# Expert outputs of the last three groups: scattered by token and loaded plainly, in place of gathers and pauses on GpSimd

## The reference, cut to what matters

```python
logits = xf @ gate_w + gate_b
probs = softmax(logits)
top2_vals, top2_idx = top_k(probs, 2)
cw = zeros((N, 8)).at[arange(N)[:, None], top2_idx].add(top2_vals)
for e in range(8):
    h = gelu(xf @ W1[e] + b1[e])
    out += cw[:, e:e+1] * (h @ W2[e] + b2[e])
```

## Time and profile before

| | |
|---|---|
| Median of 3 runs | 3025.66 us (3024.79 to 3034.64) |
| The profiled execution's own time | 3015.32 us |
| Its span, from the first to the last instruction | 3013.5 us |
| TensorE, busy | 2478.9 us, 82% of the span |
| VectorE, busy | 1969.8 us, 65% |
| ScalarE, busy | 1863.8 us, 62% |
| GpSimd, busy | 1698.9 us, 56% |
| Granted TensorE clock, mean | 0.929 of full speed |

### The profile page before, as it was taken

How to read it: one execution, slowest core, us unless ns; L and a number is a source line. 1 busy time by engine, 2 the same in 40 slices (tenths; PEclk the granted TensorE clock), 3 DMA queues, 4 the chain that set the end, 5 groups by cost and what they waited for, 6 DMA issues and landing times.

```text
span 3013.5 us, 75982 instructions
## 1 busy us (share of the span) xinstructions
PE 2478.9 (82%) x27338; PEld 1745.8 (58%) x27338; DVE 1969.8 (65%) x5155; ACT 1863.8 (62%) x3409; POOL 1698.9 (56%) x1758
## 2 busy tenths in 40 slices
PE   6898888988999888888988998888988877675720
PEld 3566556666666666566666666666666665554510
DVE  3688878887666667877777777677777775422222
ACT  3666666667776667677677677767777754432310
POOL 1224455544333334655555565555567778689986
PEclk9999999999999999899999999999999998787965
DMA  5233443336444454334433343333354443456743
GB/s 214 103 116 121 165 166 128 132 125 220 164 163 139 138 184 145 112 106 123 129 111 114 110 151 115 122 112 115 122 155 123 133 135 119 131 177 212 229 129 92
DMA packets 262562, 421.90 MB, mean 140 GB/s; under 512 B 41756, under 2 KB 141224, under 8 KB 261424
## 3 DMA queue, kind: packets, MB, share of 16 engines
q1 hardware_dynamic: 219376, 327.69, 32.0%
q0 software_dynamic: 32768, 67.17, 7.9%
q10 hardware_dynamic: 10048, 22.19, 2.3%
HBM read 198.26 MB, written 231.22 MB: 143 GB/s over the span
## 4 chain that ended last, share of the span: by engine, by line
PE 51%; ACT 18%; POOL 12%; issue 9%; DVE 5%; DMA 3%; SPq 2%; ACTq 1%; POOLq 0%; DVEq 0%
PE bank_m L844 8%; POOL yg L1238 7%; PE bank_to L768 5%; PE bank_m L836 4%; PE bank_s L808 4%; PE bank_s L736 3%; PE bank_s L814 3%; PE bank_s L723 3%; ACT pt_sb_a L1064 3%; PE bank_to L777 3%; ACT v_a L1049 2%; ACT L1194 2%; POOL xin L1248 2%; PE bank_s L746 2%; ACT p_sb_b L1069 2%
## 5 line engine op out<-in xcount | busy, mean ns | idle before, releaser
L1228 POOL DMA_INDIRECT x_sorted<-xn_c,place_i x512 | 534.3, 1044 | 338.5 <-PE bank_s L707 121.1
L1238 POOL DMA_INDIRECT yg<-y_sorted,place_i x512 | 517.0, 1010 | 277.7 <-PE bank_to L790 131.9
L1221 POOL TENSOR_TENSOR s_sb_a<-s_sb_a,mx_a 128x512 f32<-128x512 f32 x256 | 266.9, 1043 | 674.4 <-DVE mx_a L1614 674.0
L1606 DVE TENSOR_TENSOR s_sb_a<-bank_s,bias_a 128x512 f32<-128x512 f32 x256 | 176.5, 689 | 314.9 <-PE bank_s L707 219.8
L836 PE MATMUL bank_m<-xe,wk_e 128*128 128x512 f32 x552 | 276.3, 625 | 38.7 <-ACT hid L1099 29.0
L844 PE MATMUL bank_m<-wk_e,hid 128*128 128x128 f32 x2208 | 281.6, 290 | 0.9 <-ACT hid L1099 0.9
L1221 POOL TENSOR_TENSOR s_sb_b<-s_sb_b,mx_b 128x512 f32<-128x512 f32 x256 | 271.6, 1061 | 11.9 <-DVE mx_b L1614 11.9
L844 PEld LDWEIGHTS bank_m<-wk_e,hid 128*128 128x128 f32 x2208 | 275.8, 207 | 2.0 <-issue 1.9
L768 PE MATMUL bank_to<-k_consts,p_sb_b 128*128 128x128 f32 x1024 | 173.1, 293 | 103.4 <-ACT pt_sb_a L1064 68.9
L1069 ACT ACTIVATE p_sb_a<-s_sb_a 128x512 f32<-128x512 f32 x256 | 160.7, 628 | 128.4 <-POOL s_sb_a L1221 128.1
L1099 ACT ACTIVATE hid<-bank_m,wk_e 128x512 f32<-128x512 f32 x276 | 183.9, 686 | 74.1 <-PE bank_m L836 66.5
(11 more groups left out here) (222 smaller groups left out, 5920.8 us busy)
## 6 DMA issues: line engine op xcount, KB each, us to landing
y_sorted<-t_back SPq DMA_DIRECT2D x192, 512.0 KB
y_sorted<-yo SPq DMA_DIRECT2D x170, 256.0 KB
wk_e<-in_w_experts_dram SPq DMA_DIRECT2D x134, 321.0 KB
xs<-x_sorted SPq DMA_DIRECT2D x134, 256.0 KB
t_kept<-t SPq DMA_DIRECT2D x64, 256.0 KB
t_back<-t_kept SPq DMA_DIRECT2D x32, 512.0 KB
xin<-in_x_dram SPq DMA_DIRECT2D x128, 112.0 KB
x_res<-in_x_dram SPq DMA_DIRECT2D x256, 56.0 KB
```

Of the source, the lines that this page charges most:

```text
L1221: pool.tensor_tensor(s[:, :, :], s[:, :, :], m[:, :, None].to_broadcast(shape), ALU.subtract).then_inc(s_sub[w], 1)
L1228: pool.indirect_dma_start(out=x_sorted[group_of[d] % XSIDES].ap(), out_offset=bass.IndirectOffsetOnAxis(ap=place_i[:, d % KEPT, n:n + 1], ...
L1238: pool.indirect_dma_start(out=yg[:, c % 2, n, :], out_offset=None, in_=y_sorted[side].ap(), in_offset=bass.IndirectOffsetOnAxis(ap=place_i ...
L1606: tt(s_sb[0][:, :, :].rearrange("p (r h) n -> p r (h n)", h=2), scores, bias_a[:, kind, :, :].rearrange("p (r h) n -> p r (h n)", h=2), AL ...
```

## The change

Groups 0 to 2 are gathered as before. For groups 3 to 5 (images 20 to 31):

- Each token row carries a 129th column, its home: the row of its output in a new array `y_tokens`, by token and choice. `xn_c`, `x_sorted` and the loaded tiles `xs` get rows of 129 floats. VectorE writes the first choice's homes (`homes_of`), and the second choice's when the first choice's scatters have landed (`second_homes`, at steps 6 and 7). Padding rows of a tile come from a constant array `spare`, with homes in a spare part of `y_tokens`.
- ScalarE copies the homes of each slot tile to `back_to`. GpSimd's `scatter_back` writes each finished `yo` tile to `y_tokens` with four indirect DMAs of 128 rows. In the passes they stand where `BACK_AT` says (step, move); in the tail they follow one another in the order of tiles. `store_pair` does nothing for these groups. `yo` gets three buffers.
- Each image's output is then one plain load of 1 MB, `[128, 16 x 128]`, issued by SyncE in `bring_back` when all tiles of the group have landed. In the tail, four rooms hold outputs and four hold residuals; two and three of them lie over buffers of the window attention that are no longer used.

For all groups: the pauses go; the two sums in a pass are in passes 24 to 29 (as far as groups allow: passes 24, 25, 26 and 29) and images 14 to 19 are gathered from pass 29 on; `xn_b` lies over `cmp_c1`.

```diff
-PAUSE = 4
 FREE_PASSES = 1
 YSIDES = 3
-UNPAUSED = 4
+LATE = 3
...
+IDS, YO = 8, 3
...
-TWO_SUMS_FROM = 29
-PAIRS_PER_SUM = 2.5
+TWO_SUMS = range(24, 30)
+PAIRS_TO_SUM = 3
+HOME, ROW_W = D, D + 1
+MOVES = PART * SUB
+BACK_AT = (((4, 1), (4, 1), (4, 1), (4, 2), (5, 1), (5, 2), (6, 1), (6, 1)),
+           ((6, 2), (7, 1), (7, 1), (7, 2), (8, 1), (8, 1), (8, 2), (9, 1)),
+           ((9, 1), (9, 2), (10, 1), (10, 1), (10, 2), (11, 1), (11, 1), (11, 2)))
+OUT_ROWS = (4, 5, 6, 7, 0, 1, 2, 3)
...
-        while i < PASSES - FREE_PASSES and len(took) < (SUMS_PER_PASS if i >= TWO_SUMS_FROM else 1) and s < IMAGES:
+        while i < PASSES - FREE_PASSES and len(took) < (SUMS_PER_PASS if i in TWO_SUMS else 1) and s < IMAGES:
             g = group_of[s]
-            if u < len(pairs) and pairs[u].group <= g or ends.get(g, PASSES) >= i:
+            if g >= LATE or u < len(pairs) and pairs[u].group <= g or ends.get(g, PASSES) >= i:
...
+        def room_of(c):
+            if c < first_tail_sum:
+                return c % 2, 0
+            r = (c - first_tail_sum) % 4
+            return (2, 3, first_tail_sum % 2, (first_tail_sum + 1) % 2)[r], (1, 2, 3, 0)[r]
...
+        def landed(eng, k, done):
+            after(eng, y_out[k], 16 * len(range(k, min(done, late_tile), YO)))
+            after(eng, y_back[k], 16 * MOVES * sum(q >= late_tile for q in range(k, done, YO)))
+        def tiles_landed(eng, done):
+            for k in range(YO):
+                landed(eng, k, done)
...
+                    here = spare[SLOTS * e:SLOTS * e + SLOTS, :].rearrange("(p j) d -> p (j d)", p=P)
+                    eng.dma_start(rows, here).then_inc(zeroed, 16)
...
             def store_pair(u):
                 pair = pairs[u]
+                if pair.group >= LATE:
+                    return
...
+                if c == first_tail_sum:
+                    sp.wait_ge(s_added[0], IMAGES * TILES)
+                    sp.wait_ge(o_ready[0], IMAGES * TILES)
+                    sp.wait_ge(qn_ready, 4 * IMAGES)
+                    sp.wait_ge(av_ready, 3 * IMAGES)
+                if t2_uses(c):
+                    sp.wait_ge(summed, SUM_STEPS * (max(n for n in range(c) if rooms[n][1] == kept) + 1))
+                for h in range(2):
+                    sp.wait_ge(t2_out[h], 16 * (c + 1))
+                sp.dma_start(t2_home[kept].rearrange("p t d -> p (t d)"), t2_kept.ap()[c, :, :]).then_inc(t2_in[kept], 16)
+                if c >= first_late:
+                    g = group_of[c]
+                    after(sp, stored[room], 16 * IO_DMAS * y_uses(c))
+                    tiles_landed(sp, last_tile[g])
+                    at = TOP * (SPARE + TOKENS * (c - last_image[g - 1] - 1))
+                    rows = y_tokens[g].ap()[at:at + TOP * TOKENS, :]
+                    sp.dma_start(y_room[room], rows.rearrange("(p r) d -> p (r d)", p=P)).then_inc(y_in[room], 16)
...
+            at = first_tail_sum
+            for g in range(group_of[first_tail_sum], len(GROUPS)):
+                for c in range(max(first_tail_sum, last_image[g - 1] + 1), last_image[g] + 1):
+                    if c - 4 >= at:
+                        store_image(at)
+                        at += 1
+                    bring_back(c)
+                while at <= last_image[g]:
+                    store_image(at)
+                    at += 1
+            for n in range(4):
+                sp.wait_ge(stored[n], 16 * IO_DMAS * sum(room == n for room, _ in rooms))
...
+                for _, q, _ in pair.members if pair.group >= LATE else ():
+                    landed(act, (q - IDS) % YO, q - IDS + 1)
+                    func(back_to[:, q % IDS, :].rearrange("p (n j) -> p n j", n=PART), xs_b[buffer_of(q)[0]][:, :, :, HOME],
+                         ACT.Copy).then_inc(ids_kept, 1)
...
+                t, choice = OUT_ROWS[n % TILES], n // TILES
                 pool.wait_ge(gate, GATE_STEPS * (d + 1))
+                if d >= first_late:
+                    pool.wait_ge(homes_set, 3 * (d - first_late) + (1 if not choice else 2 if t >= 4 else 3))
...
+            def scatter_back(u, k):
+                _, q, _ = pairs[u].members[k // MOVES]
+                if k % MOVES == 0:
+                    pool.wait_ge(ids_kept, q - late_tile + 1)
+                    pool.wait_ge(yo_ready, q + 1)
+                j = k % MOVES
+                pool.indirect_dma_start(out=y_tokens[pairs[u].group].ap(),
+                                        out_offset=bass.IndirectOffsetOnAxis(ap=back_to[:, q % IDS, j:j + 1], axis=0),
+                                        in_=yo[:, q % YO, j, :], in_offset=None).then_inc(y_back[q % YO], 16)
...
-            pauses = itertools.count()
-            def apart():
-                n = next(pauses)
-                after(pool, paused, n)
-                pool.memset(xin[:, 0:PAUSE, :], 0.0).then_inc(paused, 1)
...
+                    for j in (i - 1, i):
+                        for slot in range(SLOTS_PER_PASS):
+                            u = slots[j][slot] if 0 <= j < PASSES else None
+                            if u is not None and pairs[u].group >= LATE:
+                                for m, when in enumerate(BACK_AT[slot][0:MOVES * len(pairs[u].members)]):
+                                    if when == (t + TILES * (i - j), k):
+                                        scatter_back(u, m)
...
-            for c in sums[PASSES - 1][1:]:
-                for k in range(12, TOP * TILES):
-                    gather(c, k)
-                    apart()
-            for c in range(first_tail_sum, IMAGES):
-                for k in range(TOP * TILES):
-                    gather(c, k)
-                    if c < IMAGES - UNPAUSED:
-                        apart()
+            for u in tail:
+                for k in range(MOVES * len(pairs[u].members)):
+                    scatter_back(u, k)
...
+            def homes_of(d, choice, tiles):
+                first = last_image[group_of[d] - 1] + 1
+                ts(xn_c[d % 2][:, tiles, HOME], const("home")[:, tiles], float(TOP * TOKENS * (d - first) + choice),
+                   None, ALU.add).then_inc(homes_set, 1)
+            def second_homes(d, h):
+                dve.wait_ge(scattered[h], 16 * (TILES * d + 4))
+                homes_of(d, 1, slice(4 * h, 4 * h + 4))
...
-                after(dve, y_out[q % 2], 16 * PART * (q // 2))
-                tt(yo[:, q % 2, :, :].rearrange("p (n j) d -> p n j d", n=PART),
+                landed(dve, q % YO, q)
+                tt(yo[:, q % YO, :, :].rearrange("p (n j) d -> p n j d", n=PART),
...
+                    if c < first_late:
+                        dve.wait_ge(gathered[room], 16 * TOP * TILES * (c // 2 + 1))
+                    else:
+                        dve.wait_ge(y_in[room], 16 * (loads_before(c) + 1))
...
+                if t >= 6 and on(d) and d >= first_late:
+                    second_homes(d, 7 - t)
```

More of the change, by code:

```diff
@@ L268, in hybrid_kernel @@
         rs_b = sb("rs_b", [P, 3, 4])
-        xn_b = sb("xn_b", [P, 4, D])
         xt_b = sb("xt_b", [P, TOKENS])
@@ L279, in hybrid_kernel @@
         rs_c = sb("rs_c", [P, 3, 4])
-        xn_c = [sb(f"xn_c{n}", [P, TILES, D]) for n in range(2)]
+        xn_c = [sb(f"xn_c{n}", [P, TILES, ROW_W]) for n in range(2)]
         xt_c = sb("xt_c", [P, TOKENS])
@@ L440, in buffer_of, with y_uses, loads_before, t2_uses @@
             return b, before + r // 6 + 1
[L442 removed]
+        tail_sums, late_sums, at = [[] for _ in tail], [], -1
         for c in range(first_tail_sum, IMAGES):
[L444 to L445 removed]
+            at = max([at + 1] + [n + PAIRS_TO_SUM for n, u in enumerate(tail) if pairs[u].group == group_of[c]])
+            (tail_sums[at] if at < len(tail) else late_sums).append(c)
+        first_late = last_image[LATE - 1] + 1
+        late_tile = last_tile[LATE - 1]
+        def room_of(c):
[3 more added lines that the diff above has]
+            return (2, 3, first_tail_sum % 2, (first_tail_sum + 1) % 2)[r], (1, 2, 3, 0)[r]
+        rooms = [room_of(c) for c in range(IMAGES)]
+        def y_uses(c):
+            return sum(rooms[n][0] == rooms[c][0] for n in range(c))
+        def loads_before(c):
+            return sum(rooms[n][0] == rooms[c][0] for n in range(first_late, c))
+        def t2_uses(c):
+            return sum(rooms[n][1] == rooms[c][1] for n in range(c))
+        def by_choice(c):
+            flat = y_room[rooms[c][0]]
+            return flat.rearrange("p (n t d) -> p n t d", n=TOP, d=D) if c < first_late else flat.rearrange(
+                "p (t n d) -> p n t d", n=TOP, d=D)
+        def landed(eng, k, done):
[4 more added lines that the diff above has]
+                landed(eng, k, done)
         block = ctx.enter_context(nc.Block())
@@ L527, in bring_back @@
             def bring_back(c):
-                after(sp, summed, SUM_STEPS * c)
-                for h in range(2):
-                    sp.wait_ge(t2_out[h], 16 * (c + 1))
```

(9 more changed lines are left out.)

113 lines of the change are left out of this document (54 added, 59 removed).

## The result

The changed kernel took 2989.17 us (median of 4 runs, 2987.10 to 2995.46), the kernel before 3025.44 (the three runs of the table and one more): a ratio of 0.9877, interval 0.9853 to 0.9901, some 36 us faster. The prediction was 2987.0. The profiled execution took 2989.77 us with a span of 2988.0.

The account below looks back on a forecast made before the run. From pass 29 on GpSimd's list of work was taken as the bound: 2246.7 + 687 + 12 of waits = 2946, plus 29 behind the last scatter = 2975, median 2987 us. Forecast 2965 to 3010 (chance 0.59); whole range 2942 to 3036.

Parts of the forecast that it names:

- GpSimd's list: GpSimd's work from 2246.7 us on: 470 indirect DMAs at 1.327, 623.7, plus 63.4 of subtractions, 687.1 against 704 before.
- Rival 1: From pass 29 on: collisions with VectorE thin out, indirect DMAs cost 1.25 us each, median 2940 us; chance 0.15.
- The waits: GpSimd's waits from pass 29 on: 2 us a pass and 2 for the last gate, 12; bounds 0 and 124.
- rival 2: Passes 29 to 33: attention and a full GpSimd hold each other up, waits 63 us, median 3038; chance 0.12.
- the 9.4 us for a pair: Tail: TensorE's time for a pair of slot tiles when nothing holds it, some 190 us for 20 pairs.
- the price without cover: Passes: VectorE waiting in `second_homes` for scatters to land, uncovered: 1.6 us twice a pass, 38 us over twelve images.
- The passes: Passes 29 to 31 were to last longer by some 18, 12 and 6 us.
- The end: After the last scatter: landing, loads hiding the first two sums, last sum and store; 29 us, range 26.3 to 34.6.
- The sum: From 2246.7 us: last scatter issued at 2946, 29 us behind it, span end 2975; 38.5 us less, median 2987.

Follow-up runs that it names:

- The pauses alone: The kernel before without its pauses on GpSimd, its gathers, loads and sums kept: 2969.07 us, 0.9813 of the kernel before.
- the sums ahead: The kernel before without pauses, with the second sum of a pass from pass 24 on instead of 29: 2961.47 us, 0.9787 of the kernel before.

## Why the prediction was right

**GpSimd's list.** The terms held almost singly: 470 indirect DMAs at 1.327 were forecast, 470 at 1.311 measured (7.4 us less in all); 63.4 us of subtractions against 61.0. The back-scatter, which no row of before showed, costs about what a gather costs: 1.032 us against 0.984 in this trace. The mean stayed at 1.31 and didn't fall to 1.25, since the collisions with VectorE stayed: beside the multiplication a scatter lasts 2.45 us, as a gather did in the earlier trace rows, where its neighbours last 0.96:

```profile
2754.43 2.28 DVE L1679 TENSOR_TENSOR v_a<-v_a,weight 128x2048 f32<-128x2048 f32 x1
```

```profile
2753.84 0.96 POOL L1320 DMA_INDIRECT y_tokens<-yo,back_to  x1 [0.30 <-issue]
2755.10 2.45 POOL L1320 DMA_INDIRECT y_tokens<-yo,back_to  x1 [0.30 <-issue]
```

The Trainium skill's GPSIMD Engine Reference, section 1. Specifications, has GpSimd contend with VectorE instructions of two SBUF inputs; the trace agrees (2.45 us against 0.96).

Rival 1 falls with the mean of 1.31. That the list is the bound is shown three ways: 32 DMAs more cost 43.5 us, 292 pauses 107, and 69 DMAs fewer give 52, where the tiles begin to set the pace.

**The waits.** 12 us were forecast, 24 measured, and they lie elsewhere. In passes 29 to 33 few are left (2.2 us for TensorE and 1.2 for the maximum are the longest), where 12 were reckoned; rival 2 wanted 51 or more. ScalarE's exponential does wait for GpSimd's subtraction there, but no more than before (74 us from pass 29 to 2640, against 75). The 18.2 for `yo` in the tail are the term that I missed: I had put TensorE at 190 us against 206 for the scatters and taken it to be always ahead. But the 9.4 us for a pair held only where nothing holds TensorE up. Ahead of GpSimd's longest wait it had stood 7.4 us for the weights of a slot tile, and 13.6 us once before:

```profile
2862.36 1.11 PE L898 MATMUL bank_m<-k_consts,kk_a 128*128 128x128 f32 x4 [7.41 <-DMA kk_a<-in_w_experts_dram]
```

```profile
2867.95 0.96 POOL L1320 DMA_INDIRECT y_tokens<-yo,back_to  x1 [7.68 <-DVE yo L1666]
```

VectorE does stand in `second_homes`, which I had put at nothing:

```profile
  DMA x_sorted<-xn_c,place_i: 48.1, 12
who waited for it (us, times):
  POOL y_tokens L1320: 0.8, 4
  POOL x_sorted L1308: 0.3, 1
```

These rows are from the view of that line (L1594), 2100 to the end: 48.1 us in 12 of its 24 executions, all of them after the start of pass 29, and more than the 38 that I named as the price without cover. It costs little all the same, since GpSimd waited 1.1 us for it.

**The passes.** Pass 29 is 97.0 us by ScalarE's copies, 13 longer than the 83.6 of before, where 18 were forecast. By GpSimd's eight subtractions for an image's window tiles (`s_sb_a`), images 29 and 30 take 104.8 and 95.5 us against 87.1 each before: 17.7 and 8.4 longer, where 18 and 12 were forecast.

**The end.** 29 us were forecast, 25.85 measured, just below my lower bound of 26.3, and made of other parts. I let the sums hide under the loads; in fact the first sum begins 6.6 us after the last scatter and all three then follow each other without a wait, so VectorE sets the end, not the DMA engines.

**The sum.** From pass 29: 687 + 12 + 29 = 728 forecast, 677.3 + 24.2 + 25.85 = 727.4 measured. So the errors, -10, +12 and -3, cancel; that the total is out by only 1 us is luck, since single terms were out by up to 12. The step to the median held as well: 38.5 us less were forecast and 36 measured.

**Where the gain comes from** the prediction left open, and the runs show it. The pauses alone are worth 57 us, the sums ahead perhaps another 8. What then still parts that kernel from the changed one, the back-scatter with its loads, buffers and rows, costs 28 (2961.5 to 2989.2). Group padding makes 276 scatters of 192 gathers, 84 more, and GpSimd is where they stand. The order matters: in the changed kernel, whose list is the bound, the sums ahead are worth 43.5. The back-scatter does keep GpSimd fed: with 401 indirect DMAs (three of four, which leaves a quarter of the rows unwritten) it needs 671.0 us from pass 29, while the gathering kernel with the sums ahead needs 700.1 with 386. So it loses by its count, not by its order; a back-scatter without padding was not run.

## What to carry to other kernels

Count the instructions that a change puts on the engine whose list is the bound, with the gaps between them, before counting the waits that it removes: here one scatter was hardly dearer than one gather, but padding made more of them. Take a change of several parts apart before keeping it, since one part (no pauses) gave more than the whole. A move off an engine is worth its full price only while that engine's list is the bound: the same 32 DMAs were worth 43.5 us in one kernel and 8 in another.

## What was unexpected

A pause of 0.54 us behind an indirect DMA costs GpSimd 0.43: around it the issue gap shrinks from 0.30 to 0.17 us. And pass 29 begins anywhere between 2246.7 and 2267.7 us in traces of kernels that do nearly the same until there: compare two profiles from a landmark that stands behind the common part, not from the start of the span.
